# GpSimd's start in attention, a third and a fourth buffer, and five reordered stretches in a graph attention and expert kernel

## The reference

```python
# layer 1: graph attention on layernorm(x), 16 heads of 32
seq = (x @ W_seq).reshape(N, H, DH)
scores = leaky_relu(score1[:, :, None] + score2[:, None, :], 0.2)   # score1 = seq.a1, score2 = seq.a2
attn = softmax(scores + (1 - adj) * -65500.0)
hidden = (attn @ seq).reshape(N, 512) @ W_out + b_out
x = x + elu(hidden)
# layer 2, on layernorm(x): shared and routed feed-forward
shared = relu2(xf @ up_w.T) @ down_w.T                # relu2(v) = max(v, 0)**2, 2048 wide
lat = xf @ fc1_w.T                                    # 256 wide
# each row goes to 2 of 8 experts, by sigmoid(xf @ gate.T) + corr_bias, inside the better group of 4
he = relu2(lat @ w1[e].T) @ w2[e].T
routed = (sum of the two he, weighted) @ fc2_w.T
x = x + shared + routed
```

## Time and profile before

| what | us |
|---|---|
| median of 3 runs | 1034.56 |
| lowest, highest of the runs | 1034.47, 1037.38 |
| the profiled execution | 1036.99 |
| its span, first to last instruction | 1035.2 |
| PE, DVE, ACT, POOL busy | 992.7, 793.9, 664.1, 263.8 |

### The profile page before, as it was taken

The page is one execution under the profiler, slowest core; times in us unless marked ns, Lnnn a source line. Parts: engine busy times, 40 slices in busy tenths (PEclk is TensorE's granted clock), DMA queues, the critical chain, the costliest instruction groups (busy, mean ns, idle before and its releaser), DMA issues.

```text
span 1035.2 us, 27169 instructions
## 1 busy us (share of the span) xinstructions
PE 992.7 (96%) x11243; PEld 881.7 (85%) x11243; DVE 793.9 (77%) x1175; ACT 664.1 (64%) x995; POOL 263.8 (25%) x312
## 2 busy tenths in 40 slices
PE   7998899999999999998988999999999989999998
PEld 6877899999999999997767888888888877778887
DVE  6789999999999999964986333457766579866554
ACT  3479999999898989714775343344455556655431
POOL 3112233344433343453431000000263000006500
PEclk9999999999999999999999999999999999999999
DMA  9931111111111111803763000110163124453242
GB/s 245 107 66 41 63 44 43 63 44 43 44 45 62 43 43 44 271 22 110 234 221 135 1 1 1 23 60 1 51 213 103 56 92 129 125 179 89 91 129 101
DMA packets 53600, 89.99 MB, mean 87 GB/s; under 512 B 5904, under 2 KB 30096, under 8 KB 52976
## 3 DMA queue, kind: packets, MB, share of 16 engines
q1 hardware_dynamic: 43104, 67.26, 19.6%
q0 software_dynamic: 7296, 12.59, 6.8%
q10 hardware_dynamic: 3088, 8.49, 2.6%
HBM read 74.82 MB, written 26.08 MB: 97 GB/s over the span
## 4 chain that ended last, share of the span: by engine, by line
PE 43%; DVE 4%; DMA 2%; ACT 2%; issue 1%; POOL 1%; SPq 0%; DVEq 0%; ACTq 0%; POOLq 0%
PE bank L1365 17%; PE bank L1832 16%; PE bank L1909 2%; DMA xs<-sorted_latent_rows 2%; PE bank L691 1%; PE bank L1860 1%; PE bank L1861 1%; PE bank L1863 1%; PE bank L1817 1%; DMA xr<-in_x 1%; PE bank L1815 1%; DVE hid L1156 1%; DVE hid L1159 1%; PE bank L1853 1%; PE bank L1814 1%
## 5 line engine op out<-in xcount | busy, mean ns | idle before, releaser
L753 ACT ACTIVATE arena<-arena 128x1024 fp8e4<-128x1024 f32 x320 | 336.9, 1135 | 2.4 <-ACT arena L745 1.4
L1007 PE MATMUL bank<-arena 128*128 128x132 f16 x4096 | 283.5, 220 | 12.1 <-DVE arena L853 6.4
L1007 PEld LDWEIGHTS bank<-arena 128*128 128x128 fp8e4 x4096 | 244.4, 97 | 13.9 <-DVE arena L853 7.4
L1365 PE MATMUL bank<-xt,up_parts 128*128 128x512 f32 x768 | 187.9, 394 | 2.1 <-DVE up_parts L1349 2.1
L1832 PE MATMUL bank<-down_parts,h_parts 128*128 128x512 f32 x768 | 184.5, 389 | 0.0
L1011 PE MATMUL bank<-arena 128*128 128x66 f16 x4096 | 172.4, 195 | 0.0
L1365 PEld LDWEIGHTS bank<-xt,up_parts 128*128 128x128 f32 x768 | 143.4, 189 | 31.4 <-issue 2.1
L1832 PEld LDWEIGHTS bank<-down_parts,h_parts 128*128 128x128 f32 x768 | 143.9, 188 | 30.0 <-issue 0.2
L824 DVE TENSOR_SCALAR arena<-arena 128x1024 uint8<-128x1024 f32 x192 | 169.3, 948 | 0.0
L1011 PEld LDWEIGHTS bank<-arena 128*128 128x128 fp8e4 x4096 | 153.5, 98 | 0.0
L1339 DVE TENSOR_TENSOR relu_sb<-relu_sb 128x512 f32<-128x512 f32 x64 | 44.3, 692 | 119.9 <-ACT relu_sb L1314 119.8
(11 more groups left out here) (244 smaller groups left out, 1381.2 us busy)
## 6 DMA issues: line engine op xcount, KB each, us to landing
arena<-s_rows SPq DMA_DIRECT2D x32, 512.0 KB, 3.7
sorted_latent_rows<-zeros SPq DMA_DIRECT2D x1, 4992.0 KB, 18.2
xs<-sorted_latent_rows SPq DMA_DIRECT2D x39, 128.0 KB, 2.1
sorted_expert_rows<-expert_y SPq DMA_DIRECT2D x39, 128.0 KB, 1.7
arena<-in_adjT POOLq DMA_DIRECT2D x8, 512.0 KB, 27.1
xr<-in_x SPq DMA_DIRECT2D x16, 256.0 KB, 4.7
x_rows<-hid SPq DMA_DIRECT2D x16, 256.0 KB, 4.2
up_sb<-in_upT ACTq DMA_DIRECT2D x4, 1024.0 KB, 5.5
```

Of the source, the lines that this page charges most:

```text
L753: last = nc.scalar.activation(m8[:, k, j, :], s1b[:, k % 2, :], ACT.Sigmoid, bias=bias_now[:, k % 2, j:j + 1], scale=STEEP, saturate=False)
L1007: last = nc.tensor.matmul(o, m8[:, k, j, i * P:(i + 1) * P], vs[:, b, j, :], start=(j == 0), stop=(j == T - 1))
L1365: last = nc.tensor.matmul(bank[6 + s % 2][:, :], sa[:, s % 2, a, k, :], xt[c][:, b, k, :], start=(i == 0), stop=(i == len(mm) - 1))
```

## The change

GpSimd's turn in attention waits for DVE's compare of its turn k - 1 (`dve_compared`), and for nothing else ahead of `combine`. The largest score's transposition and spreading and the first degrees go ahead of `project(7)`, in another bank, and DVE's second `any_neighbour` goes behind `scale_columns`. `hn` has three buffers and is filled one tile further ahead; the first weight parts of the shared layer are made by ACT one tile earlier. `xs` has four buffers, the third eviction is split around the second expert tile's low part, and the parts of weights for steps 49 and 51 that aren't needed until the experts are over move into the expert loop.

```diff
-        TOP_BANK = bank[4]
+        TOP_BANK = bank[6]
@@ exponents
-                step(nc.vector.tensor_copy(topr[:, 0:H], TOP_BANK[:, P:P + H]))
+                nc.vector.tensor_copy(topr[:, 0:H], TOP_BANK[:, P:P + H]).then_inc(topr_ready, 1)
+                dve.wait_ge(topr_ready, 2)
@@ setup_dve
-            any_neighbour(1)
             apply_empty_rows((0, 1))
             scale_columns()
+            any_neighbour(1)
@@ largest_scores
-                pe.wait_ge(st_copied, 5)
+                pe.wait_ge(s_ready, 1)
@@ degrees
                 pe.wait_ge(any_ready, half + 1)
+                pe.wait_ge(topr_ready, 2)
@@ setup_pe
             project(6)
+            largest_scores()
             scores_to_rows()
-            largest_scores()
-            project(7)
             spread_largest()
             degrees(0)
+            project(7)
@@ normalise
-            if t >= 2:
-                pool.wait_ge(ht_in_psum, t - 1)
+            if t == 2:
+                pool.wait_ge(wo_low, 1)
+            if t >= 3:
+                pool.wait_ge(ht_in_psum, t - 2)
@@ attention, GpSimd's body
-                        pool.wait_ge(m_ready, 4 * p + k + 3)
-                        pool.wait_ge(unit_in_psum, 4 * p + k + 1)
+                        pool.wait_ge(dve_compared, 4 * p + k + 4)
@@ project_act
-                if t == T - 1:
+                elu_parts(t)
+                if t == T - 2:
                     act.wait_ge(up_loaded, 16 * KD)
                     ...
                     high_a(act, 0)
                     high_a(act, 1)
-                elu_parts(t)
@@ project_pool
-                if 3 <= t < T:
-                    normalise(pool, t)
+                if t == 3:
+                    normalise(pool, 3)
+                if 3 <= t < T - 1:
+                    normalise(pool, t + 1)
                 if t >= 3:
                     root(t - 3)
@@ load_xs (four buffers)
-                    if i >= 3:
-                        sp.wait_ge(xs_in_psum, i - 2)
+                    if i >= 4:
+                        sp.wait_ge(xs_in_psum, i - 3)
@@ ACT, unit(s)
+                    if s == 3 * FS + 1:
+                        return
                     high_b(act, s)
@@ ACT, expert loop
+                    if i == 3:
+                        high_b(act, 3 * FS + 1)
@@ DVE, unit(s)
                     if s == 3 * FS + 1:
                         low_xs(0)
-                    if s % FS == 1:
+                        evict(2, range(2))
+                        low_xs(1)
+                        evict(2, range(2, TT))
+                    elif s % FS == 1:
                         evict(s // FS - 1)
                     ...
+                    if s == 3 * FS + 1:
+                        return
                     if s + 2 < STEPS:
                         low_a(dve, s + 2)
                     low_b(dve, s)
@@ DVE, expert loop
-                    if i + 3 < TILES:
+                    if -2 < i and i + 3 < TILES:
                         low_xs(i + 3)
+                    if i == 4:
+                        low_a(dve, 3 * FS + 3)
+                        low_b(dve, 3 * FS + 1)
```

More of the change, by code:

```diff
@@ L614, in build @@
         ones_r = place("ones_r", 28656, [P], f32r)
-        hn = place("hn", 28928, [2, D])
+        hn = [place(f"hn{b}", o, [D]) for b, o in enumerate((28928, 29440, 28032))]
         hT = place("hT", 24832, [2, 2, KD, P], f32r)
@@ L662, in normalise @@
             pool.wait_ge(rden_ready, 1 if t < IT else 2)
-            if t >= 2:
-                pool.wait_ge(ht_in_psum, t - 1)
-            nc.gpsimd.tensor_tensor(hn[:, t % 2, :].rearrange("p (h d) -> p h d", h=H), hid[:, t, :, 0:DH],
+            if t == 2:
+                pool.wait_ge(wo_low, 1)
+            if t >= 3:
+                pool.wait_ge(ht_in_psum, t - 2)
+            nc.gpsimd.tensor_tensor(hn[t % 3].rearrange("p (h d) -> p h d", h=H), hid[:, t, :, 0:DH],
                                     rden[:, t, :].rearrange("p (h o) -> p h o", o=1).to_broadcast([P, H, DH]),
@@ L679, in transpose_h @@
             for k in range(KD):
-                last = nc.tensor.transpose(bank[6 + t % 2][:, k * P:(k + 1) * P], hn[:, t % 2, k * P:(k + 1) * P], ident2)
+                last = nc.tensor.transpose(bank[6 + t % 2][:, k * P:(k + 1) * P], hn[t % 3][:, k * P:(k + 1) * P], ident2)
             last.then_inc(ht_in_psum, 1)
@@ L1262, in build @@
         ORDER = (0, 1, 4, 5, 6, 7, 2, 3)
-        xs = place("xs", 41216, [3, LAT])
+        xs = [place(f"xs{b}", o, [LAT]) for b, o in enumerate((41216, 41472, 41728, 8192))]
         xsT = place("xsT", 41984, [2, 2, KL, P], f32r)
@@ L1294, in build @@
         pair_high, pair_ready = sem("pair_high"), sem("pair_ready")
-        xs_loaded = [sem(f"xs_loaded{b}") for b in range(3)]
+        xs_loaded = [sem(f"xs_loaded{b}") for b in range(4)]
         y_stored = [sem(f"y_stored{b}") for b in range(3)]
@@ L1395, in load_xs @@
                 def load_xs(i):
-                    if i >= 3:
-                        sp.wait_ge(xs_in_psum, i - 2)
-                    sp.dma_start(xs[:, i % 3, :], xs_dram[i * P:(i + 1) * P, :]).then_inc(xs_loaded[i % 3], 16)
+                    if i >= 4:
+                        sp.wait_ge(xs_in_psum, i - 3)
+                    sp.dma_start(xs[i % 4], xs_dram[i * P:(i + 1) * P, :]).then_inc(xs_loaded[i % 4], 16)
                 def load_base(u):
@@ L1557, in step, with evict @@
                     dve.wait_ge(dve_step, steps[0])
-                def evict(c):
+                def evict(c, tiles=range(TT)):
                     dve.wait_ge(x1_loaded[c % 2], 16 * (c // 2 + 1))
-                    for t in range(TT):
+                    for t in tiles:
                         if t < TT - 1:
@@ L1848, in transpose_xs @@
                 def transpose_xs(j):
-                    pe.wait_ge(xs_loaded[j % 3], 16 * (j // 3 + 1))
+                    pe.wait_ge(xs_loaded[j % 4], 16 * (j // 4 + 1))
                     if j >= 1:
@@ L1852, in transpose_xs @@
                     for k in range(KL):
-                        last = nc.tensor.transpose(T1[:, k * P:(k + 1) * P], xs[:, j % 3, k * P:(k + 1) * P], ident3)
+                        last = nc.tensor.transpose(T1[:, k * P:(k + 1) * P], xs[j % 4][:, k * P:(k + 1) * P], ident3)
                     last.then_inc(xs_in_psum, 1)
```

## The result

The changed kernel took 1025.36 us in the median (1023.84 to 1026.85) against 1035.41 for the kernel before, run beside it: 10 us faster. The ratio on record is 0.989, interval [0.987, 0.991]; the quotient of the two medians is 0.990. Forecast were 1028.0 in a range from 1021 to 1033, faster with a chance of 0.80.

The account below looks back on a forecast made before the run. DVE was taken to set attention's pace, PE being full too. Terms -1.2 (setup), -2.5 (attention), -3.2 (projection), -0.3 (experts) sum to -7.2 us: median 1034.56 to 1027.4, given as 1028; range 1021 to 1033.

Parts of the forecast that it names:

- So its copy comes about 2.5 us earlier: Setup: DVE no longer waits 2.52 us for the spreading behind project(7), so its copy comes at 55.5; term -1.2 us.
- rival (1): Attention: GpSimd gets ahead of mask_own too, or a second L949 does, in every unit; 13 us price, 1043 us; chance 0.08.
- I count six such gaps: Attention: six waits of PE for DVE's low parts, 198 to 431 us, 4.9 us in all; first closes, five shrink 0.41.
- the wait ahead of it only shifts: Attention: PE's wait at its fourth unit, 2.74 us, ahead of the clock's fall, moves without changing size.
- The dip of the clock stays in the sum: Attention: the granted clock's fall behind PE's fourth unit (mean 0.86 for 12 us) remains, so no gain was counted.
- rival (3): Attention: all gaps close (-4.9) and the shorter wait at the fourth unit spares the clock's fall; -11.2, 1023 us; chance 0.12.
- Between 127 and 198 us PE sets the pace: Attention: in that stretch PE, not DVE, was taken as the bound.
- 12 x 4.38 = 52.6 against 52.8: -0.2: Projection: the twelve tiles after tile 3 stay at 4.38 us, DVE's 3.65 plus 0.73 from GpSimd; only 0.2 us gained.
- Rival (2): Projection runs free: GpSimd's and DVE's phases drift apart and PE's 3.86 us decides; 6 us more, 1022 us; chance 0.12.
- come as much earlier: Projection's end: without DVE's 1.15 us wait, the last residual, root and norm come as much earlier; -1.0 us (0 to -1.2).
- PE goes on some 1.1 us earlier: Experts' start: of PE's 2.25 us wait for the second transposition's low part, about 1.1 goes; experts' term -0.3 us.
- its 0.59 us at 862.23 stay (3.6 us in four such waits): Experts' loop: the fourth xs buffer does nothing, as loads are issued behind a result's store; PE's xs waits remain.

Follow-up runs that it names:

- the four kernels with the old code: The kernel before, and it with the setup's, attention's or projection's edits alone; PE's xs waits 3.6, 1.4, 2.0 and 2.4 us.
- the six with the new code, four buffers and the old order of loads: Experts' edits alone, the changed kernel, and four one-edit variants of it; xs waits 2.9, 0.7, 2.6, 1.3, 2.8 and 2.4 us.
- the eleven kernels with the same order of loads: Four kernels with old expert code, six with the fourth xs buffer, and the changed kernel with three xs buffers (1025.29 us); xs waits 0.7 to 3.6 us.
- the first four experiments: The kernel before with one group of edits each: setup 1035.04 us, GpSimd's wait in attention 1033.99, projection with high_a 1030.36, experts 1036.14.

## Why the prediction was right, and where it was not

The parts in the traces, with the forecast's terms:

| | forecast | measured | |
|---|---|---|---|
| setup | -1.2 | -1.98 | |
| attention | -2.5 | -1.57 | |
| projection | -3.2 | -4.5 to -4.9 | |
| experts | -0.3 | -0.8 | xs waits taken out |
| sum | -7.2 | -8.9 to -9.3 | medians: -10.0 |
| only in the two profiles | | -1.3, -2.9 | start, xs waits |

**Setup.** The mechanism held and the size was off in two steps. "So its copy comes about 2.5 us earlier" left out that largest_scores moves too: DVE's idle time ahead of the first maximum (1.53 us) goes as well, and of the 2.52 only 1.12. "Which is 0.5 us after DVE's exponents would be ready" was wrong: L448 needs only the first four of the eight matmuls of degrees(0) and follows the exponents without a gap (55.64). Then "it comes perhaps 0.3 us earlier" of ACT's last copy: it came 0.6 us earlier, net, and DVE's products at 83.63 1.8.

**Attention.** The compares, the held mask, the untouched mask_own and the pair of 46.6 us came as written, and rival (1) did not. ("0.41 instead of 0.39 to 0.57" misread its own row: 6.39 - 5.69 is 0.70. The sum of 5.31 us has it right.) The term was too large because of "I count six such gaps". Five are DVE's: the first did not close, it shrank by 0.54, and the others by 0.45. The sixth, in the middle of a unit, the trace names "issue" both before (0.84) and after (0.95); it is PE's own. Behind the fifth PE does not wait for DVE any more: from there to the end of attention it takes 82.7 us before and 82.8 after, at PE's pace. And "the wait ahead of it only shifts" missed that the mask at the fourth unit would be a held one, 0.45 us. "The dip of the clock stays in the sum" was right for the sum and wrong in its reason, and so was the half of rival (3) that would spare it: PE's slow matmuls cost nothing either way while DVE has no idle time. "Between 127 and 198 us PE sets the pace" failed there too: PE had no wait in that stretch because it was making up its lag, but DVE's end was already fixed.

**Projection.** Tile 3's -2.0 was 2.4. The term that was mis-sized is "12 x 4.38 = 52.6 against 52.8: -0.2". The pitch of 4.38 came, to the hundredth, but only from the fourth of the twelve tiles on: the first three run at PE's 3.87, which is 3 x 0.52 = 1.5 us, and the last two together take 8.43, 0.3 less than two pitches. That DVE's lag has to use up the tile held ahead in the buffers first would explain them, but no run varies the number of buffers alone, and the kernel before had two fast tiles in the same place. Rival (2) was true for three tiles. The tail gave 0.35 and not 1.0: the step "come as much earlier" took a wait of DVE's for one of the chain.

**Experts.** 2.1 us at the start, 1.1 back at i = 4 (forecast 1.1 and most of 1.2), and the fourth buffer does nothing, as argued. So "PE goes on some 1.1 us earlier" is the term that was mis-sized: the whole wait went, and nothing of it is left for the eviction that still stands ahead. From xs(0) to xs(38), less the waits for xs, it is 78.6 us in the mean of the four kernels with the old code and 77.8 in the six with the new code, four buffers and the old order of loads: 0.8, where single traces lie up to 0.6 from these means. What failed is "its 0.59 us at 862.23 stay (3.6 us in four such waits)": such waits lie between 0.7 and 3.6 us in the eleven kernels with the same order of loads, and the profile of before had drawn the largest.

**The sum** was 2 us short, and the difference of the medians is 2.8 more than it. Three terms were too small and one too large, and that attention's error (0.9) and the setup's (0.8) cancel is luck. "The runs of before lie at either 1034.5 or 1037" did not hold either: its 34 runs beside the first four experiments spread over all of 1033.2 to 1039.5, and their median is 1036.5.

## What to carry to other kernels

Before pricing a wait, find the engine that has no idle time in the stretch: while the others still wait for it further on, a wait of another engine, or its lower clock, is free, and only what that engine gives up counts. Where two engines contend, the moment at which the second is woken decides what it lands on, and a single semaphore moved by one instruction was worth 0.2 to 0.6 us a pair. Where buffers run ahead of a bottleneck, ask whether the first tiles go at the faster engine's pitch (three did here); and compare profiles from a mark ahead of the edits, with waits for small loads taken out.

## What was not expected of the hardware

- A GpSimd instruction that already stands in a DVE instruction over the shared pair is done sooner than one that is woken by a semaphore at that instruction's end: two L953 were over 1.09 to 1.10 us behind the mask, two L949 1.42 to 1.70. The next compares took 6.10 and 4.46 us instead of 6.39 and 4.63, beside the same work.
- The same GpSimd instruction (128x512, two operands) took 1.05 us beside DVE subtractions that read PSUM, and 1.59 beside two that read SBUF alone, one of which grew from 0.69 to 1.42.
- Behind a wait of 1.9 us in the shared layer the next twelve matmuls took 4.25 to 4.58 us in six profiles, at a mean granted clock of 0.53 to 0.73 in their first 3 us, and 2.97 to 3.01 in eight, at 1.00, behind the same wait in the same stage.
- Code that no edit touches begins up to 4 us apart in different executions (40.8 to 44.8 us), and loads of 128 KB made PE wait 0.7 to 3.6 us. Together with the third group's clock these are of the size by which the runs of one kernel differ; how much of that spread they make up was not shown.
